# The fused stage of a two-layer transformer kernel: transposed scores made by TensorE, maxima subtracted in PSUM

## What is computed

```python
a = softmax(Q @ K.T / sqrt(8))        # per sequence and head, 64 x 64, not causal
x = x + (a @ V) @ wo + bo             # Q, K, V are projections of layer-normed inputs
out = x + gelu(LN(x) @ w1 + b1) @ w2 + b2
```

## Time and profile before

| | us |
|---|---|
| three runs: median (lowest to highest) | 1391.83 (1389.43 to 1393.59) |
| the profiled execution | 1399.14 |
| its span, first to last instruction | 1397.3 |
| busy in the span: TensorE / VectorE / ScalarE / GpSimd | 1242.1 / 953.1 / 988.4 / 899.7 |
| fused stage, start to first scores | 914.9 to 964.4 |
| fused stage, first scores to last residual | 964.4 to 1265.0 |
| final MLP | 1265.0 to the end |

### The profile page before, as it was taken

The page is one execution under the profiler, slowest core; times in us unless marked ns, Lnnn a source line. Parts: engine busy times, 40 slices in busy tenths (PEclk is TensorE's granted clock), DMA queues, the critical chain, the costliest instruction groups (busy, mean ns, idle before and its releaser), DMA issues. The chain is left out here.

```text
span 1397.3 us, 59862 instructions
## 1 busy us (share of the span) xinstructions
PE 1242.1 (89%) x23050; PEld 1031.0 (74%) x23050; DVE 953.1 (68%) x2152; ACT 988.4 (71%) x1972; POOL 899.7 (64%) x1432
## 2 busy tenths in 40 slices
PE   4999999989999998958999999985878788788997
PEld 2777877777878887837999999953666666665775
DVE  3888888876787886594555555546889999854331
ACT  1778777767888887346787776624988888865553
POOL 2577777776677665216999998767677777413331
PEclk9999999999999999579999999997999999999999
DMA  4233343322222220051222222243222222112221
GB/s 125 77 108 117 110 126 106 114 86 86 83 82 83 82 76 26 16 136 39 69 65 68 66 67 67 66 143 103 63 68 68 73 73 73 41 49 61 68 74 39
DMA packets 137984, 109.81 MB, mean 79 GB/s; under 512 B 16928, under 2 KB 113696, under 8 KB 137888
## 3 DMA queue, kind: packets, MB, share of 16 engines
q1 hardware_dynamic: 129440, 91.22, 22.1%
q0 software_dynamic: 8448, 17.32, 5.2%
HBM read 74.35 MB, written 34.08 MB: 78 GB/s over the span
## 5 line engine op out<-in xcount | busy, mean ns | idle before, releaser
L907 DVE TENSOR_REDUCE at_mx<-at_ps_s 128x16 f32<-128x1024 f32 x128 | 156.0, 1220 | 91.9 <-PE at_ps_s L587 47.2
L813 ACT ACTIVATE at_pt<-at_ps_t 128x1024 f32<-128x1024 f32 x128 | 130.6, 1020 | 55.3 <-PE at_ps_t L608 54.5
L2357 POOL DMA_INDIRECT ex_xg<-x,ex_ti x136 | 146.3, 1076 | 23.5 <-issue 21.9
L806 ACT ACTIVATE at_pr<-at_dd 128x1024 f32<-128x1024 f32 x128 | 135.2, 1056 | 34.7 <-DVE at_dd L915 34.6
L2471 DVE COPY ex_wt<-experts 128x1156 f32 x133 | 102.7, 772 | 80.4 <-DVE ex_y L2477 74.4
L2429 ACT ACTIVATE ex_hg<-ex_ps_h,ex_wt 128x128 f32<-128x128 f32 x544 | 154.6, 374 | 1.2 <-PE ex_ps_y L2388 1.2
L915 DVE TENSOR_TENSOR at_dd<-at_ps_s,at_mx 128x1024 f32<-128x1024 f32 x128 | 153.7, 1202 | 0.1
L2379 PE MATMUL ex_ps_h<-ex_xt,ex_wt 128*128 128x128 f32 x1088 | 146.5, 278 | 1.0 <-ACT ex_xt L2421 0.8
L2016 POOL DMA_INDIRECT l_yg<-rows,l_sl x128 | 125.8, 983 | 31.9 <-issue 29.4
L608 PE MATMUL at_ps_t<-ident,at_pr 128*128 128x128 f32 x1024 | 140.0, 280 | 6.0 <-issue 5.4
L2388 PE MATMUL ex_ps_y<-ex_wt,ex_hg 128*128 128x128 f32 x1088 | 143.6, 275 | 0.4 <-ACT ex_hg L2429 0.4
(11 more groups left out here) (264 smaller groups left out, 3166.5 us busy)
## 6 DMA issues: line engine op xcount, KB each, us to landing
rows<-ex_y SPq DMA_DIRECT2D x136, 64.0 KB
x<-at_ln_out SPq DMA_DIRECT2D x32, 256.0 KB, 3.2
at_kx<-in_xt SPq DMA_DIRECT2D x16, 256.0 KB, 2.8
at_qx<-in_xt SPq DMA_DIRECT2D x16, 256.0 KB, 2.8
at_vin<-in_xt SPq DMA_DIRECT2D x16, 256.0 KB, 2.8
at_xr<-in_x SPq DMA_DIRECT2D x16, 256.0 KB, 3.0
cx<-in_ctx SPq DMA_DIRECT2D x16, 256.0 KB, 3.2
x1t<-at_xt SPq DMA_DIRECT2D x16, 256.0 KB, 3.3
```

The lines of the kernel that those rows point to most:

```text
L806: act.activation(pr[:, p], dd[:, p], ACT.Exp, scale=SCALE).then_inc(p_ready, 1)
L813: act.activation(pt[:, 2 * h + p], ps_t[:, :, :, :], ACT.Copy).then_inc(pt_ready, 1)
L907: dve.tensor_reduce(mx[:, p], ps_s[:, :, 4 * p:4 * p + 4, :], AX.X, ALU.max).then_inc(mx_ready, 1)
L2357: pool.indirect_dma_start(out=xg[:, s, :], out_offset=None, in_=x_src, in_offset=bass.IndirectOffsetOnAxis(ap=ti[:, s:s + 1], axis=0)).the ...
```

## The change

The stage goes by units now: four per group, unit i is half h = i // 2 and row groups 2 rp and 2 rp + 1 with rp = i % 2. Scores are made twice by TensorE: once as before (ps_s, now two banks, one buffer) for the maxima alone, and once transposed (ps_t, four banks, two buffers), with K and Q swapped. The transposed ones of a unit are issued in the `scores` block of the unit behind it. VectorE takes the maxima (16 per partition), splits each into three bf16 parts (two small subtractions, each waiting for the one before), TensorE turns the parts with one bf16 product (`turn_largest`), VectorE copies half of the partitions back to SBUF as bf16 (`copy_largest`, placed behind the next unit's maximum), TensorE subtracts them in PSUM with eight bf16 products of 32 rows (`take_largest`), and ScalarE's exponential reads PSUM and writes pt. `subtract`, `turn` (32 transposes per group), `copy_t` and the buffers dd and pr are gone. `mask_k` leaves ScalarE: kb is cleared once and Sync fills it from zt with eight transfers per half group, 16 partitions each, in pieces of 64 floats; the bias of K is added in `keep_k`. `mask_q` and `copy_v` are split by halves. All orders are rewritten; GpSimd's gathers keep their number. V of groups 8 to 15 is staged in x3, FinalStage's buffers lie in pt.

```diff
-        dd = n.sb("dd", [P, 2, 4, 4, SEQ])
-        pr = n.sb("pr", [P, 2, 4, 4, SEQ])
+        kb = n.sb("kb", [P, 2, QB, 2, SEQ])
+        qb = n.sb("qb", [P, 2, QB, 2, SEQ])
+        mx = n.sb("mx", [P, 2, P])
+        mt = n.sb("mt", [P, P], BF16)
+        minus = n.sb("minus", [P, QB, P], BF16)
-        ps_s = n.ps("ps_s", [P, 4, 2 * QB, SEQ])
-        ps_t = n.ps("ps_t", [P, 2, 4, P])
+        ps_s = n.ps("ps_s", [P, 2, 2 * QB, SEQ])
+        ps_t = n.ps("ps_t", [P, 2, 2, QB, P])
...
+                def mask_k(a, h):
...
+                        sp.wait_ge(s_ready, 4 * a.g + 2 * h - 1)
+                    for j in range(2):
+                        for r in range(4):
+                            heads = slice(32 * r + 16 * j, 32 * r + 16 * j + 16)
+                            sp.dma_start(kb[heads, h, :, j, :],
+                                         zt[heads, bass.ds(a.place * GT + GT // 2 * h, GT // 2)].rearrange(
+                                             "p (b s) -> p b s", b=QB)).then_inc(in_k[h], 16)
...
+                def scores(a, i):
...
+                    if own and beyond(n, 0):
+                        pe.wait_ge(mx_ready, n)
...
+                    if last and beyond(n, 2):
+                        pe.wait_ge(pt_ready, n - 2)
                     for b in range(QB):
+                        if own:
+                            for r in range(2):
+                                rows = slice(64 * rp + 32 * r, 64 * rp + 32 * r + 32)
+                                mm = pe.matmul(ps_s[:, r, 2 * b:2 * b + 2, :], qb[rows, h, b, :, :], kb[rows, h, b, :, :],
+                                               start=(b == 0), stop=(b == QB - 1), skip_group_check=True)
+                        if last:
+                            for r in range(2):
+                                rows = slice(64 - 64 * rp + 32 * r, 64 - 64 * rp + 32 * r + 32)
+                                mm = pe.matmul(ps_t[:, 1 - rp, r, b, :], kb[rows, before_h, b, :, :],
+                                               qb[rows, before_h, b, :, :], start=(b == 0), stop=False,
+                                               skip_group_check=True)
...
+                def turn_largest(a, i):
+                    pe.wait_ge(parts_ready, n + 1)
+                    if beyond(n, 0):
+                        pe.wait_ge(pt_ready, n)
...
+                def take_largest(a, i):
+                    pe.wait_ge(mc_ready, n + 1)
+                    for b in range(QB):
+                        for r in range(2):
+                            rows = slice(64 * rp + 32 * r, 64 * rp + 32 * r + 32)
+                            mm = pe.matmul(ps_t[:, rp, r, b, :], minus[rows, b, :], mt[rows, :], start=False,
+                                           stop=(b == QB - 1), skip_group_check=True)
+                    mm.then_inc(t_ready, 1)
...
+                def exponent(a, i):
+                    act.wait_ge(t_ready, n + 1)
...
+                    act.activation(pt[:, h, :, 2 * rp:2 * rp + 2, :].rearrange("p b r q -> p r b q"), ps_t[:, rp],
+                                   ACT.Exp, scale=SCALE).then_inc(pt_ready, 1)
...
+                def split(a, i):
+                    dve.wait_ge(mx_ready, n + 1)
+                    dve.tensor_tensor(largest(rp, 1), largest(rp, 0), high(rp, 0), ALU.subtract).then_inc(rest_ready, 1)
+                    dve.wait_ge(rest_ready, n + 1)
+                    dve.tensor_tensor(largest(rp, 2), largest(rp, 1), high(rp, 1), ALU.subtract).then_inc(parts_ready, 1)
+                def copy_largest(a, i):
+                    dve.wait_ge(mt_ready, n + 1)
...
+                    dve.tensor_copy(mt[half, :], ps_t[half, 1 - rp, 0, 0, :]).then_inc(mc_ready, 1)
```

More of the change, by code:

```diff
@@ L1463, in fused_phase @@
         z4t_ready, qx_ready = n.sem("z4t_ready"), n.sem("qx_ready")
-        in_v, v_out = n.sem("in_v"), n.sem("v_out")
+        in_v, v_out = [n.sem(f"in_v{i}") for i in range(2)], n.sem("v_out")
         early_k, early_v = n.sem("early_k"), n.sem("early_v")
@@ L1479, in fused_phase, with largest, high @@
         zt = layer.out_tr
-        bank = [ps_s[:, i].rearrange("p a b -> p (a b)") for i in range(4)]
+        bank = [ps_s[:, i].rearrange("p a b -> p (a b)") for i in range(2)] + [
+            ps_t[:, 0, i].rearrange("p b q -> p (b q)") for i in range(2)]
+        whole = pt.rearrange("p h b r q -> p (h b r q)")
         def staged(g):
[L1484 to L1487, removed]
+            return (whole[:, bass.ts(g, GT)] if g < NG // 2 else x3[:, g].rearrange("p t d -> p (t d)"))
+        def largest(rp, part):
+            return mx[:, rp, 64 * rp:64 * rp + 64].rearrange("p (r x) -> p r x", r=2)[:, :, 8 * part:8 * part + 8]
+        def high(rp, part):
+            return mx[:, rp, 64 * rp:64 * rp + 64].bitcast(BF16).rearrange("p (r x t) -> p r x t", r=2, t=2)[
+                :, :, 8 * part:8 * part + 8, 1]
         def held(a):
@@ L1551, in scores @@
                         pe.wait_ge(kt_ready, NG)
                         pe.wait_ge(vt_ready, NG)
+                    if last and beyond(n, 2):
+                        pe.wait_ge(pt_ready, n - 2)
                     for b in range(QB):
-                        t = SEQ * (QB * h + b)
-                        for r in range(4):
-                            rows = slice(32 * r, 32 * r + 32)
-                            mm = pe.matmul(ps_s[:, r, 2 * b:2 * b + 2, :], qb[rows, QB * h + b, :, :],
-                                           kb[rows, :, t:t + SEQ], start=(b == 0),
-                                           stop=(b == QB - 1 and not causal), skip_group_check=True)
@@ L1560, in scores @@
-                    if causal:
-                        for f in range(2):
-                            for r in range(4):
-                                rows = slice(32 * r, 32 * r + 32)
-                                mm = pe.matmul(ps_s[:, r, :, 32 * f:SEQ], c.pick[rows, f, :],
-                                               c.hide[rows, f, None, 32 * f:SEQ].broadcast_to(
-                                                   [32, 2 * QB, SEQ - 32 * f]),
-                                               start=False, stop=(f == 1), skip_group_check=True)
@@ L1951, in step @@
                         normalise(a.shift(-1), 1)
+                    if a.unrolled and -3 <= g < -1:
+                        for e in ((5, 6, 7, 8), (11, 12, 13, 14, 15))[g + 3]:
+                            keep_v(e)
+                    if a.shift(2).exists():
+                        gain_own(a.shift(2))
+                    if a.exists():
+                        maximum(a, 3)
+                        copy_largest(a, 2)
+                        split(a, 3)
                     if a.shift(2).exists():
```

316 lines of the change are left out of this document (149 added, 167 removed).

## The result

| | before | after |
|---|---|---|
| median of 4 runs | 1392.28 us | 1489.90 us |
| lowest to highest | 1389.43 to 1393.59 | 1486.10 to 1491.57 |
| ratio to before | | 1.0700 (95%: 1.0674 to 1.0727) |
| profiled execution, span | 1397.3 us | 1488.0 us |
| mean granted clock | 0.967 | 0.94 |

The change made the kernel 98 us slower, outside the predicted range (1364 to 1403) by 87 us. One execution of a later kernel, e9_moments_back, took 4103 us, far from its other three, and is left out of its figures.

What follows compares the result with a forecast made beforehand. No engine was free, VectorE led, and the chain per unit was to set the period. Filling -0.6, steady -9.2 and emptying -5.5 gave -15.3 us: 1384 profiled, 1377 us as median (7 lower), range 1364 to 1403.

Steps and rivals of the forecast that it cites:

- GpSimd moves nothing new: Claim that the change gives GpSimd no new transfers; its own queue stays at 16.6 us per group.
- the change leaves its work as it is: Claim on GpSimd, called a second floor that busy shares hide: its work stays the same.
- the walk: Step following one group's new order through the engines: 16.85 us plus 0.3 for GpSimd's input, 17.2 against 18.1 before.
- TensorE's work is unchanged: Per-group sum for TensorE: fewer transposes against added scores, turns and subtraction products, net -0.1 us.
- VectorE's sum: Per group, four subtractions lost (4.9 us), tiny subtractions and half copies gained (2.6): net -2.3 us.
- 15.8 - 5.5 = 10.3: ScalarE per group: four passes and two maskings lost (-5.8 us), 0.3 added for split copies of V and q.
- TensorE's subtraction block: Cost of eight bf16 subtraction products on TensorE: 0.35 us taken, ends 0.2 and 0.7.
- rival B: Dearer hand-offs: subtraction blocks 0.65 us, semaphores 0.1 more, 18.4 us per group, 1396 us; chance 0.20.
- Sync's queue: Sync's 16 key transfers per group, 0.42 us each with gap, 6.2 us per half, hidden in their window.
- rival C: Late keys: 0.67 us per key transfer makes 18.8 us per group, 1405 us; chance 0.13.
- The filling: Stretch from the stage's first scores, 63.3 us before: forecast -0.6 us, with scores 2 us earlier and low clock costing 6.
- The emptying: Stage's last part, without the front's work: 50.6 us against 56.1, -5.5 us.

Runs made afterwards that it cites:

- e9_moments_back: Changed kernel with `next_statistics` and `front_moments` put back ahead of `maximum(a, 3)`: 1498.97 us, ratio 1.0783.
- e1: Changed kernel with all eight gathers of group g+4 issued in one step of GpSimd, none left for the next: 1432.91 us, ratio 1.0285.
- e2: Changed kernel with VectorE's `weigh_first` moved behind `residual` and `weigh_second` behind `split(a, 2)`, GpSimd's order kept: 1439.99 us, ratio 1.0336.
- e11: e10 with the masked keys written by ScalarE in place of Sync's 16 transfers per group: 1415.74 us, ratio 1.0189.
- e3: Changed kernel with Sync's 16 key transfers per group replaced by four masked copies of ScalarE: 1489.29 us, ratio 1.0690.
- e10: e1 with `add_bias` ahead of `front_rstd` and `normalise(g-1, 0)` behind `split(a, 1)`: 1421.72 us, ratio 1.0227.
- e6: e1 with a second buffer for ot, which needs a TensorE loop over pairs of groups: 1458.93 us, ratio 1.0468.
- e7: e1 and e3 together, with two ot buffers, TensorE's loop over pairs and the second half's keys copied behind exponential 3: 1440.69 us, ratio 1.0334.
- e5: Kernel before with only `next_statistics` and `front_moments` moved behind the next two maxima and subtractions: 1497.67 us, ratio 1.0746.
- e8: e7 with GpSimd's `add_bias` moved ahead of `front_rstd`: 1437.23 us, ratio 1.0305.

## Why the prediction was wrong

**The step that failed** is the one that costs GpSimd: "GpSimd moves nothing new" and, above, "the change leaves its work as it is". Both are true of the work and useless for the time. I counted GpSimd as a floor of 16.6 us and gave it an input at 12.95 in the walk, but I never followed its output: the three gathers of the group before, which stand behind `front_rstd`, and `weigh_first`, which waits for all eight. The change moved VectorE's half of that ring (`gain_own`, statistics, moments) towards the end of the step while `weigh_first` stayed at its front, and the ring went from 16.6 to 24.1 us. One line of arithmetic on the earlier trace rows would have been enough to suspect it: GpSimd waits only 1.5 us per group, so whatever shifts its inputs by more must shift its gathers. Cutting the ring gave back 57 us at one place (e1) and 50 at the other (e2). The other 40 us are no single step: e11, with two more moves and the keys on ScalarE, gave back 17 of them, and what is left is below.

**The walk's 17.2 us per group.** With the rings opened it is 18.4 (e11). The walk let TensorE wait 3.7 us and so work 13.15; it was busy 14.2 (102.01 / 132 x 18.4). That is near the 14.4 of the earlier trace rows and fits the term "TensorE's work is unchanged", so the walk seems to have left out about 1 us of the work that the sum had kept. Whether this is all of the missing 1.2 us wasn't tried. It also left out that `normalise` waits for the projection two groups back.

**VectorE's sum was right.** The groups of small operations in the changed kernel (count, busy, mean ns), beside the earlier trace rows:

```profile
L1870 DVE CAST l_mt<-l_ps_t 64x128 bf16<-64x128 f32 x33 | 9.4, 284 | 0.5
...
L1859 DVE TENSOR_TENSOR l_mx<-l_mx 128x16 f32<-128x16 f32 x33 | 6.9, 208 | 0.5
...
L1861 DVE TENSOR_TENSOR l_mx<-l_mx 128x16 f32<-128x16 f32 x33 | 5.8, 175 | 1.1
```

Together 0.67 us per unit; I took 0.65. The -2.3 per group nearly held (14.7 in e11 against 16.8).

**ScalarE** was off by 1.5 us: 11.8 us per group (105.90 / 217.39 x 24.15), where 15.8 - 5.5 = 10.3 was forecast. The exponential from PSUM took 1.02, as taken. The split of the query masks was too cheap: four of 0.56 where there were two of 0.77 (the view of the earlier trace rows), +0.7, and the split copies of V four of 0.41 where there were two of 0.62, +0.4; I had allowed 0.3 for both. The remaining 0.7 wasn't traced. It cost nothing, as ScalarE isn't a bound.

**TensorE's subtraction block** (0.35, with ends at 0.2 and 0.7). TensorE's timeline of the changed kernel:

```profile
1117.02 0.40 PE L1614 MATMUL l_ps_t<-l_mt,l_minus 32*128 32x128 bf16 x8 [0.23 <-DVE l_mt L1870]
1117.25 0.37 PE L1593 MATMUL l_ps_t<-l_qb,l_kb 32*128 32x128 f32 x1
```

The eight products show 0.40 us, and the next scores start 0.23 behind their start. The near end was right, and rival B's 0.65 is out. The sum by the figure of the Trainium skill (TensorE: Matmul & The Clock Gate, Back-to-back issue gap), 0.65 too, is out with it. B's other half, dearer semaphores and a strict order, may be where e11 ends; that its 18.4 us per group is B's figure is luck, as the 1.2 us of the dearer block in it didn't come.

**Sync's queue** (0.42 per key transfer, ends 0.38 and 0.64). A burst of eight takes 5.15 to 5.89 us, so 0.64 to 0.74 each: the far end or beyond. By rival C's own formula 0.65 would have decided (18.5 us per group). Without gathers the distances of 17.6 us in the last groups, with bursts 8.95 us apart (1282.94, 1291.89), look like it, but they are not: with the keys on ScalarE these groups are no closer (18.3 in e3, and 17.60 and 17.52 in e11 where e10 has 17.58 and 17.53). e3 shows that the transfers made no difference to the changed kernel, and e10 against e11 (6 us, the intervals just overlap) that some 0.4% hangs on them once the ring is open; only with the longer loop (e6 against e7) were they worth 18 us.

**The filling** (-0.6) came out at +36.5. The first scores start at 971.9, 7.5 us later than before instead of 2 earlier, and 92.3 us lie between them and y(1), where it was 63.3; the granted clock over them is 0.72 (0.87 in the earlier trace rows), the lower of its two levels for a good part. Most of this is the ring, which turns in the filling too: e11 has 10.6 us left of it, 4.6 of them ahead of its first scores (969.0). Counted from the stage's first product it is more: 48.5 us to the first scores before (915.88 to 964.36), 57.7 in the changed kernel (914.16 to 971.9), 58.2 in e11 (910.76 to 969.0); the phases ahead of the stage took 5.1 us less in that execution of e11, which no run explains. TensorE waits there for ScalarE's scaling of the first group:

```profile
957.58 1.08 PE L1641 MATMUL l_ps_g<-ident,l_z 128*128 128x128 f32 x4 [3.92 <-ACT l_z L1757]
```

```profile
963.76 1.09 PE L1663 MATMUL l_ps_g<-ident,l_z 128*128 128x128 f32 x4 [10.66 <-ACT l_z L1787]
```

The first row is of before, the second of e11; e1 waits 10.68, and e5, the kernel before with later moments, 8.16. So this too looks like the order of the front's work and not like set-up: that ends at 917.7 in the changed kernel, 1 us ahead of VectorE's first copy of V, and its cost of 0 was right. The prediction also misread the clock: a mean of 0.51 is the lower level nearly throughout those 18 us (0.50 in each slice of 3 us from 960 to 975), not half of the time, and TensorE was busy 9.0 us in them and not some 12. No run shows the 6 us for it as a term of its own.

**The emptying** (-5.5) was +0.3, and +1.8 in e11: the groups without gathers ran at 17.6 us, where the walk had let them shrink.

**The chances.** I gave 0.23 to slower, on 18.4 and 18.8 us per group. The two slower rivals were about costs that grew; none was about an order that closes a ring, and the range had no room for it.

## What to carry to other kernels

Before an instruction is moved in a software pipeline, follow what it releases on each other engine all the way back to its own queue, and sum the ring's length against the period. A ring of 16.6 us under a period of 18.1 shows in no busy share and in no wait at its own end, and with the ring stretched to 24.1 us the kernel lost 98 us, 57 of which came back when it was cut. Where a stage is slower with every engine less busy, read one period of the chain of waits and look for the instruction that comes back; its distance is the period. Then cut the ring at two different places, for a fault that both cuts mend is the ring's and no queue's. A move in another kernel that costs as much (e5) proves nothing until its waits show the same ring.

## What the hardware showed that I had not expected

- A VectorE subtraction of 16 elements per partition took 1.63 us in place of 0.18 while GpSimd added the bias from SBUF, and ended with it (1121.45 and 1121.41); with the two moved apart (e10) it took 0.24 at most. I had counted GpSimd and VectorE as independent.
- A TensorE loop over pairs of groups, otherwise with the same work per group, stood 3.8 to 5.0 us without a named cause once per turn (e6, e7, e8). e6 executes 62584 instructions and e1 62626, but the instruction queue moved 111 packets and not 61.
- Transfers inside SBUF of 16 KB, as 64 pieces of 256 bytes, took Sync's queue 0.64 to 0.74 us each, nearly twice a store of 256 KB (0.38 to 0.42).
- The granted clock was lower where TensorE stalled: 1.00 in the steady part of before (TensorE busy 79%), 0.91 in the changed kernel's (67%), 0.68 up to its first store of y (56%; 0.81 and 74% before), and 1.00 again in e11 (77%).
